# Two-layer attention and FFN kernel: the FFN weights arrive already turned and are unpacked and added late in layer 0; x loads first, on the sync queue

## The reference

```python
x = x + L0_xattn(layernorm(x), ctx)   # 8 heads of 8, band of +-64 around the diagonal,
                                      # then relu(o) * ctx and a 64x64 channel mix
x = x + L0_ffn(layernorm(x))          # one 256x256 matrix, scaled; tanh-bounded row norm
x = x + L1_xattn(layernorm(x), ctx)   # rotary q and k, full 256x256 scores
x = x + L1_ffn(layernorm(x))          # 256 -> 1024 -> 256
```

```python
dequant4bit(q, scale) = (q - 7.5) * repeat(scale, 64, axis=1)     # q holds integers 0 to 15
w_up = dequant4bit(w_up_q, w_up_scale).T                          # [256, 1024]
y1 = x1 @ w_up + b_up + x1 @ w_up_lora_a @ w_up_lora_b            # rank 16
w_down = dequant4bit(w_down_q, w_down_scale).T                    # [1024, 256]
y2 = relu(y1) @ w_down + b_down + relu(y1) @ w_down_lora_a @ w_down_lora_b
```

## Time and profile before

| | us |
|---|---|
| timed runs, lowest, median, highest | 1427.28, 1429.04, 1431.03 |
| profiled execution, first to last instruction | 1429.4 |
| PE busy | 1315.2 (92%) |
| DVE, ACT, POOL busy | 955.8, 874.6, 716.5 |
| first projection matmul of layer 0 starts | 22.38 |
| first exponential of layer 0 starts | 90.79 |
| layer 0 FFN begins | about 600 |
| first projection matmul of layer 1 starts | 658.24 |
| layer 1 FFN begins | about 1195 |

### The profile page before, as it was taken

The page is one execution under the profiler, slowest core; times in us unless marked ns, Lnnn a source line. Parts: engine busy times, 40 slices in busy tenths (PEclk is TensorE's granted clock), DMA queues, the critical chain, the costliest instruction groups (busy, mean ns, idle before and its releaser), DMA issues.

```text
span 1429.4 us, 37785 instructions
## 1 busy us (share of the span) xinstructions
PE 1315.2 (92%) x11332; PEld 910.0 (64%) x11332; DVE 955.8 (67%) x2156; ACT 874.6 (61%) x1909; POOL 716.5 (50%) x1292
## 2 busy tenths in 40 slices
PE   1999999999999998882799999999999989999998
PEld 1666777777777776571466666666666655766675
DVE  6438878787888787468888888888888872111110
ACT  1147676666666667563488888888888875122211
POOL 6336777777777776404555655656656511010000
PEclk9869999999999999995799999999999999999999
DMA  8314444444344443001434444444444410000000
GB/s 243 78 36 95 103 100 90 96 100 100 90 96 100 100 90 87 6 12 37 92 91 104 105 95 103 103 97 104 102 97 107 93 41 1 15 30 15 15 15 29
DMA packets 90797, 111.18 MB, mean 78 GB/s; under 512 B 15056, under 2 KB 82384, under 8 KB 83056
## 3 DMA queue, kind: packets, MB, share of 16 engines
q1 hardware_dynamic: 83184, 103.38, 31.9%
q10 hardware_dynamic: 7552, 7.02, 1.7%
HBM read 16.52 MB, written 4.19 MB: 14 GB/s over the span
## 4 chain that ended last, share of the span: by engine, by line
PE 62%; POOL 11%; issue 11%; DVE 8%; ACT 2%; ACTq 1%; DMA 1%; POOLq 1%; SPq 1%; DVEq 1%
PE bank L459 10%; PE bank L420 8%; PE bank L652 8%; PE bank L643 8%; PE bank L436 7%; PE bank L418 5%; PE bank L470 4%; DVE row_max L1031 3%; PE bank L501 3%; POOL rot L1216 2%; PE bank L614 2%; POOL Qp L1205 2%; PE bank L490 1%; POOL k_rest L1221 1%; POOL q_rest L1201 1%
## 5 line engine op out<-in xcount | busy, mean ns | idle before, releaser
L1031 DVE TENSOR_REDUCE row_max<-bank 128x2 f32<-128x384 f32 (+1 forms) x1024 | 599.6, 617 | 148.5 <-PE bank L420 146.8
L687 ACT ACTIVATE probs<-bank 128x384 f32<-128x384 f32 (+1 forms) x1024 | 534.4, 542 | 161.8 <-PE bank L436 155.0
L420 PE MATMUL bank<-Ks,Qs 96*128 96x192 bf16 (+1 forms) x2048 | 372.1, 264 | 13.5 <-DMA Ks<-Ks 8.4
L436 PE MATMUL bank<-Qs,Ks 128*128 128x192 bf16 (+1 forms) x2048 | 367.1, 261 | 13.6 <-ACT probs L687 12.5
L1234 POOL TENSOR_SCALAR_AFFINE_SELECT probs<-probs 128x256 f32<-128x256 f32 (+1 forms) x512 | 257.2, 526 | 175.1 <-ACT probs L687 156.3
L420 PEld LDWEIGHTS bank<-Ks,Qs 96*128 96x128 bf16 x2048 | 189.3, 99 | 122.8 <-issue 37.8
L459 PE MATMUL bank<-probs,V 128*32 128x192 f32 (+1 forms) x4096 | 249.0, 361 | 3.7 <-POOL probs L1234 2.4
L436 PEld LDWEIGHTS bank<-Qs,Ks 128*128 128x128 bf16 x2048 | 188.9, 98 | 40.1 <-ACT probs L687 23.9
L418 PE MATMUL bank<-band,ident 128*128 128x384 bf16 x512 | 169.2, 331 | 1.0 <-ACT out_bias L840 0.5
L459 PEld LDWEIGHTS bank<-probs,V 128*32 128x32 f32 x4096 | 107.4, 109 | 82.7 <-issue 41.8
L1171 DVE TENSOR_TENSOR X<-bank,X 128x256 f32 (+1 forms) x32 | 13.6, 425 | 184.6 <-PE bank L652 184.6
(11 more groups left out here) (128 smaller groups left out, 1776.9 us busy)
## 6 DMA issues: line engine op xcount, KB each, us to landing
Ks<-Ks SPq DMA_DIRECT2D x64, 576.0 KB
Qs<-Qs SPq DMA_DIRECT2D x128, 192.0 KB
Qs<-Qp SPq DMA_DIRECT2D x192, 64.0 KB
Ks<-Kp SPq DMA_DIRECT2D x192, 64.0 KB
side<-in_ctx SPq DMA_DIRECT2D x64, 128.0 KB, 2.0
X<-in_x ACTq DMA_DIRECT2D x4, 1024.0 KB, 10.4
out<-X SPq DMA_DIRECT2D x8, 512.0 KB, 2.9
Qs<-max_rows SPq DMA_DIRECT2D x128, 12.0 KB
```

What stands on the lines that cost most here:

```text
L420: last = nc.tensor.matmul(dst[:, blk * win:(blk + 1) * win], Qs[0:SHIFT_ROW, pair[1], h, blk * P:(blk + 1) * P], Ks[0:SHIFT_ROW, pair[1], ...
L436: last = nc.tensor.matmul(dst[:, blk * win:(blk + 1) * win], Ks[:, pair[1], h, blk * P:(blk + 1) * P], Qs[:, pair[1], h, start(blk):start( ...
L687: nc.scalar.activation(probs[:, h % 8, 0:2 * win], exp_bank[h % 2][:, 0:2 * win], ACT.Exp, scale=SCALE).then_inc(s["exped"], 1)
L1031: nc.vector.tensor_reduce(row_max[:, pair[1], h, :], bank_of(pair, h)[:, 0:2 * win].rearrange("p (b k) -> p b k", b=2), AX.X, ALU.max).the ...
```

## The change

1. **Loads.** SP issues the first quarter of x, then the layer 0 attention weights, `ident` and `band`, then the other three quarters. ACT issues the low-rank factors and the layer 1 attention weights at the start, and `rope`, `ff0_w`, `ff0_scale`, and the packed FFN weights with their scales only after bodies 0, 1 and 2 of layer 0. The packed weights come already turned from the host, and the scales already repeated to full size (1 MB each).
2. **Table.** ACT runs a one-column square root at once, so that its table is there.
3. **Constant rows of `Ks`.** A DMA on the ACT queue from an input `minus` takes the place of POOL's memset.
4. **Low-rank products.** PE computes them alone, straight into the orientation of `up_w` and `down_w`: eight blocks of 512 columns, two before the first projection and two after each of the bodies -3, -2 and -1. ACT copies each block.
5. **Dequantisation.** DVE does eight blocks of 512 columns, two after each of the bodies 27 to 30, each in one instruction. POOL adds them to `up_w` and `down_w`, two after each of the bodies 28 to 31; the scaling of `ff0_w` moves to body 27. DVE waits for the last of these additions before the layer 0 FFN.

```diff
@@ sync
+            load_x(0)
             e.dma_start(att_w[0][:, :, :], a["att_w0"]).then_inc(weights0_in, 16)
             ...
-            e.dma_start(att_w[1][:, :, :], a["att_w1"]).then_inc(consts_in, 16)
-            e.dma_start(att_b[1][:, :], a["att_b1"]).then_inc(consts_in, 16)
-            e.dma_start(rope[:, :, :], a["rope"]).then_inc(consts_in, 16)
+            for c in range(1, X_CHUNKS):
+                load_x(c)
             e.wait_ge(cleared_q, 3)
-            e.wait_ge(cleared_k, 2)
+            e.wait_ge(minus_in, 16)
@@ tensor_prepare
-                    nc.tensor.matmul(dst, down_f[:, blk, hb * P:(hb + 1) * P], ident[:, :], start=True, stop=False)
-                    nc.tensor.matmul(dst, lora_in[:, T + hb * P:T + (hb + 1) * P],
-                                     lora_out[:, FF + blk * P:FF + (blk + 1) * P],
-                                     start=False, stop=True).then_inc(prep_ps, 1)
             ...
+                if job < 4:
+                    blk, half = job // 2, job % 2
+                    last = nc.tensor.matmul(dst[:, :], lora_in[:, blk * P:(blk + 1) * P],
+                                            lora_out[:, half * 512:(half + 1) * 512], start=True, stop=True)
                 else:
+                    for k in range(2):
+                        hb = 2 * (job - 4) + k
+                        last = nc.tensor.matmul(dst[:, k * T:(k + 1) * T],
+                                                lora_in[:, T + hb * P:T + (hb + 1) * P],
+                                                lora_out[:, FF:FF + T], start=True, stop=True)
+                last.then_inc(prep_ps, 1)
@@ scalar_loads(e, n), called first in scalar_prepare
+            if n == 0:
+                rope, ff0_w, ff0_scale
+            if n == 1:
+                e.dma_start(up_raw, a["up_q"].rearrange("(b p) n -> p b n", p=P)).then_inc(ffn_in, 16)
+                e.dma_start(up_f, a["up_scale"].rearrange("(b p) n -> p b n", p=P)).then_inc(ffn_in, 16)
+                e.dma_start(up_b[:, :], a["up_b"]).then_inc(ffn_in, 16)
+            if n == 2:
+                down_raw, down_f, down_b in the same way
@@ scalar
-            for c in range(X_CHUNKS):
-                e.dma_start(X[:, c * EARLY:(c + 1) * EARLY, :], ...
-                if c == 0:
-                    scalar_loads(e)
+            lora_in, lora_out, att_w[1], att_b[1]
+            e.wait_ge(cleared_s, 1)
+            nc.scalar.activation(gain[:, 0:1], gain[:, 0:1], ACT.Sqrt).then_inc(table_in, 1)
+            e.wait_ge(cleared_k, 1)
+            e.dma_start(Ks[SHIFT_ROW:SHIFT_ROW + PARTS, :, :, :] ..., a["minus"]).then_inc(minus_in, 16)
+            scalar_prepare(e, -AHEAD - 1)
@@ dequantise, on DVE after bodies 27 to 30
-            engine.tensor_scalar(dst, raw, 7.5, None, ALU.subtract).then_inc(signal, 1)
-            ...
-            engine.tensor_tensor(flat, flat, scale ... broadcast ..., ALU.mult).then_inc(signal, 1)
+            nc.vector.scalar_tensor_tensor(out=flat, in0=raw.rearrange("p a b -> p (a b)")[:, at_], scalar=7.5,
+                                           in1=flat, op0=ALU.subtract, op1=ALU.mult).then_inc(dequant, 1)
@@ pool_prepare, after bodies 28 to 31
+                for block in range(2 * (n - 1 - DEQUANT_FROM), 2 * (n - DEQUANT_FROM)):
+                    e.wait_ge(dequant, block + 1)
+                    nc.gpsimd.tensor_tensor(flat, flat, src...[:, at_], ALU.add).then_inc(ffn_ready, 1)
@@ gpsimd, start
-            nc.gpsimd.memset(Ks[SHIFT_ROW:SHIFT_ROW + PARTS, ...], MINUS_ONES).then_inc(cleared_k, 1)
@@ vector, ahead of the layer 0 FFN
+            e.wait_ge(ffn_ready, PREP_BLOCKS)
```

More of the change, by code:

```diff
@@ L593, in _ @@
+                last.then_inc(prep_ps, 1)
+                e.wait_ge(prep_read, PREP_BLOCKS + 2)
         @block.tensor
         def _(e):
+            e.wait_ge(lora_loaded, 2 * 16)
+            tensor_prepare(e, -AHEAD - 1)
             e.wait_ge(weights0_in, 2 * 16)
@@ L968, in vector_prepare @@
         def vector_prepare(e, n):
-            if n == -AHEAD:
-                dequantise(e, nc.vector, down_f, down_raw, down_scale, 2 * FF // QBLOCK, dequant_down)
+            if DEQUANT_FROM <= n < DEQUANT_FROM + PREP_BLOCKS // 2:
+                if n == DEQUANT_FROM:
+                    e.wait_ge(ffn_in, FFN_LOADS * 16)
+                for block in range(2):
+                    dequantise(e, 2 * (n - DEQUANT_FROM) + block)
             c = n + AHEAD + 1
@@ L1114, in _ @@
         def _(e):
+            nc.vector.memset(gain[:, 0:1], 1.0).then_inc(cleared_s, 1)
             nc.vector.memset(Ks[:, :, :, :].rearrange("p a h t -> p (a h t)").bitcast(i32), 0).then_inc(cleared_k, 1)
@@ L1274, in pool_prepare @@
         def pool_prepare(e, n):
-            if n != -AHEAD:
-                return
-            dequantise(e, nc.gpsimd, up_f, up_raw, up_scale, HB * T // QBLOCK, dequant_up)
-            for blk in range(2):
-                nc.gpsimd.tensor_tensor(ff0_w[:, blk, :], ff0_w[:, blk, :], ff0_scale[:, :],
-                                        ALU.mult).then_inc(ff0_scaled, 1)
+            if n == DEQUANT_FROM:
+                e.wait_ge(ffn_in, FFN_LOADS * 16)
+                for blk in range(2):
+                    nc.gpsimd.tensor_tensor(ff0_w[:, blk, :], ff0_w[:, blk, :], ff0_scale[:, :],
+                                            ALU.mult).then_inc(ff0_scaled, 1)
+            if DEQUANT_FROM < n <= DEQUANT_FROM + PREP_BLOCKS // 2:
+                for block in range(2 * (n - 1 - DEQUANT_FROM), 2 * (n - DEQUANT_FROM)):
+                    e.wait_ge(dequant, block + 1)
+                    dst, src = (up_w, up_f) if block < 4 else (down_w, down_f)
+                    at_ = slice(block % 4 * 512, (block % 4 + 1) * 512)
+                    flat = dst[:, :, :].rearrange("p a b -> p (a b)")[:, at_]
+                    nc.gpsimd.tensor_tensor(flat, flat, src.rearrange("p a b -> p (a b)")[:, at_],
+                                            ALU.add).then_inc(ffn_ready, 1)
         @block.gpsimd
@@ L1289, in _ @@
             nc.gpsimd.memset(V[:, :, :, :, HD:HD + 1], 1.0).then_inc(cleared_q, 1)
[L1291 to L1295 removed]
             pool_attention(e, 0, pool_prepare)
+            e.wait_ge(rope_in, 16)
             pool_attention(e, 1)
```

130 lines of the change are left out of this document (59 added, 71 removed).

## The result

The changed kernel takes 1412.53 us (median of four runs, 1410.64 to 1414.5) against 1429.88 for the kernel before on the same chip: a ratio of 0.9885, 95% interval 0.9865 to 0.9906, so 17.35 us faster. The forecast was 1400 with a range up to 1411. The direction was right, the size was not: 28.9 us were forecast. The profiled execution spans 1410.9 us, 18.5 less than the one before; what follows is worked out on these two.

What follows compares the result with a forecast made beforehand. PE bounds layer 0's bodies, and its low-rank weight work at a lower clock delays body 0. Gain 43.7 less 4, 3, 5.3 and 2.5 is 28.9 us, from 1429.4 to 1400.5, said as 1400; range 1386 to 1411.

Steps and rivals of the forecast that it cites:

- The start: Everything before body 0: it starts at 45.8 instead of 89.54, a gain of 43.7 us.
- the late loads: Layer 0 weights loaded after bodies 0 to 2: 4 us for ACT's issues, 3 for contention with layout transfers.
- the end of layer 0: Last bodies of layer 0: a loss of 5.3 us by DVE's blocks and 2.5 by POOL's additions.
- body -1 with its extra: Between first scores and body 0: 10.8 us for body -1, then 4.0 for two low-rank blocks and out_bias.
- a halved pace: Layout transfers while weights come, as queues alternate by packet: the upper half of the contention term, 3 us between 0 and 8.
- DVE's blocks: Dequantisation after bodies 27 to 30: 1.3 us each without cover before the turn of the maxima, 5.3 us in all.
- The near doubling of this term: End of layer 0: if DVE and POOL exclude each other in SBUF, the 5.3 us for DVE would near double.
- POOL's additions: After bodies 28 to 31: mostly in gaps between masks, but those after body 31 delay the last mask, 2.5 us.
- The first: Rival, chance 0.14: spare time of ACT and POOL takes the late work in layer 0, total 1384 us.
- The second: Rival, chance 0.12: the start becomes a chain of transfers, body 0 some 7 us longer, end at 1409 us.
- the third: Rival, chance 0.03: PE's lower clock stays through layer 0's first bodies, about 13 us more each; six give 1478.
- The fourth: Rival, chance 0.05: PE still waits in the start for ACT's low-rank copies or SP for minus; 1405 to 1415 us.

Runs made afterwards that it cites:

- the run without both: The changed kernel with neither DVE's eight dequantisation blocks nor POOL's eight additions, so the last FFN uses the low-rank products alone; 1399.75 us, ratio 0.9802.
- the kernel with all of it in the loop: The changed kernel with weights and scales as 32 transfers of 128 KB on SP, and dequantisation and additions by 256 columns in loop bodies; 1391.03 us.
- the experiment: The changed kernel with the constant rows of Ks written by POOL's memset as before instead of the transfer; 1413.27 us, ratio 0.9866.

## Why the prediction was wrong

Up to the first projection of layer 1 the forecast was a gain of 28.9 us, and 17.6 were measured. The start is 0.8 short (42.95 at pair 1), the late loads cost 15.3 instead of 7, and the end of layer 0 cost 10.1 instead of 7.8.

- **The start** was nearly right in its sum: 43.7 us forecast, 42.6 measured. The projection came at 14.2 and not 12.2. I said that the low-rank blocks and their copies fit ahead of it because their inputs are first on their queue; those landed only at 8.88, and the second copy ended at 13.3, after the variance was there. From projection to scores the forecast was 17.8 and 0.9 for the x load, and it took 18.7; body -1 with its extra came out at 14.0 against 14.8, which offset part of the late projection.
- **The late loads** are the step that failed. I took 3 us for the transfers, between 0 and 8, and 4 for ACT's issues. Of the 15.3 us measured, 1.6 are there without them, the issues cost 1 to 2, and the transfers, with what the clock adds, some 12, beyond the upper bound. That bound was read from single landings (2.0 and 6.8 us), as though one transfer would be late once in each of two bodies. In fact a chain of them is late in each: q's layout, then k's, the row maxima queued behind both, the replication. And the stops of over 3 us were each followed by a slower clock: 0.89 and 0.79 in the windows. The sentence that drew on the Trainium skill (DMA: Bandwidth & Descriptors, "Queues, rings and completion order": a DMA engine alternates between queues by packet) led to a halved pace while weights come. The trace agrees as far as it can show it: q's three transfers, issued from 81.96, had landed only at 91.86, 9.9 us later, where the same body of the kernel before needed at most 4.8 (121.93 to 126.71). I had that rule and kept the small value.
- **DVE's blocks**: 5.3 forecast, 4.6 measured (5.6 when read against the run without both). Right, and at the place named: PE waits 5.4 us for the maxima with the blocks alone and 2.1 without both, from 480 to 645 us. A block took 0.83 us beside the masks, where 0.66 was reckoned. The near doubling of this term that the prediction held possible did not come, though the masks were stretched.
- **POOL's additions** are the second step that failed: 2.5 forecast, 5.1 measured. Only the last mask was counted, and that part held: its wait was 3.8 instead of 1.76, 2.1 us. What was left out is the rest; with the additions alone, 2.2 us of it lie in a stretch at a mean clock of 0.68 instead of 1.00. The stretched masks are not this part, since they stretch with DVE's blocks alone. Where the additions were moved beside DVE's split, the two engines do hold each other up: a DVE operation of 0.17 us lasts 1.20 beside an addition of 512 columns and 0.66 beside one of 256. This agrees with the skill's rule that the two exclude each other (the Trainium skill, SBUF — State Buffer, "SBUF: two separate sides"). One of the two operations held at 525 us has a single input, so these rows are not only the case of two inputs that the prediction named.
- **The rivals.** The first (late work hides) is nearly what the kernel with all of it in the loop does, and not this change. The second (a start that is a chain of transfers) didn't happen: body 0 to the next row maxima took 16.9 us. The clock was back some 4 us after the first scores (a pair of L429 took 0.53 us at 33.20 and 0.33 at 37.36), so the third fell as argued. The fourth (a start that still waits) names the time that was measured, 1405 to 1415, but not its cause: the start gave 42.6 us, and only 2.0 went to a late projection.

Left open are why the loss by the same late loads varied from 6.7 to 13 us between kernels, what made the clock fall in the last bodies with POOL's additions, and which transfer of the chain is the one that counts.

## What to carry to other kernels

Moving work from the start into a steady loop is worth it only in pieces that fit the loop's gaps: 4 MB in two lumps cost some 12 us, in 32 pieces on the other queue nothing. Price a bulk load by the chain of small transfers that shares its engines, not by the mean DMA share or by one late landing. And put a block on DVE or POOL where neither the next engine nor the other of the two waits; an addition moved by one place only changed who waited.

## What the runs showed of the hardware

- A backlog holds the issuing engine: one issue of 11.16 us and one of 5.11 on ACT, behind 3 and 4 MB issued on its own queue and with the x load in flight. The seven issues just ahead of them took 0.35 to 0.49.
- POOL's memset of three partitions (5.21 us) stopped DVE's small scalar operations, for 3.51 us in the kernel before and 3.37 in the experiment, but not the three two-input operations just ahead of them (0.17 each).
- POOL's addition of two SBUF tiles (1.24 us) held a DVE operation of 0.17 us to 1.20, in the kernel with moved additions.
- Half the late bytes cost 2.0 us where all of them cost 12.4.
